# A Mamba and mixture-of-experts block: the experts' up product evicted by ScalarE and multiplied by GpSimd

## The reference, cut to what matters

```python
def reference(x, ...):            # x: (8, 1024, 256) float32
    # attention slot: a Mamba block on layernorm(x)
    xz = rms_norm(xn) @ in_proj_w; xb, z = split(xz)
    xc = silu(causal_conv4(xb) + conv_b)                     # 512 channels
    dt, B, C = split(xc @ x_proj_w); dt = softplus(dt @ dt_proj_w + dt_proj_b)
    h = exp(dt * A) * h + dt * B * xc                        # 16 states a channel, scanned over 1024 steps
    y = (sum_s(h * C) + xc * D) * silu(z)
    x = x + layernorm(y @ out_proj_w + residual)
    # FFN slot: 16 experts (256 -> 128 -> 256), 4 of 16 chosen by groups, weights sum to 1
    t = layernorm(x)
    g = einsum('th,eih->tei', t, gate_proj); u = einsum('th,eih->tei', t, up_proj)
    act = silu(g) * u
    y = einsum('teh,te->th', einsum('tei,ehi->teh', act, down_proj), combine)
    return x + layernorm(y)
```

## Time and profile before

| | us |
|---|---|
| median of 3 runs | 2711.35 |
| the profiled execution | 2710.63 |
| its span in the trace | 2708.8 |
| VectorE busy | 2437.7 |
| TensorE busy (matmul) | 2403.0 |
| ScalarE busy | 1632.9 |
| GpSimd busy | 1509.4 |

### The profile page before, as it was taken

How to read it: one execution, slowest core, us unless ns; L and a number is a source line. 1 busy time by engine, 2 the same in 40 slices (tenths; PEclk the granted TensorE clock), 3 DMA queues, 4 the chain that set the end, 5 groups by cost and what they waited for, 6 DMA issues and landing times.

```text
span 2708.8 us, 27117 instructions
## 1 busy us (share of the span) xinstructions
PE 2403.0 (89%) x8416; PEld 1179.6 (44%) x8416; DVE 2437.7 (90%) x3236; ACT 1632.9 (60%) x3312; POOL 1509.4 (56%) x546
## 2 busy tenths in 40 slices
PE   5556898999989899998989999898999989898988
PEld 2112354544535454443545445353544535443554
DVE  3999999999999999999999999999999999999642
ACT  5566566566766656666665666666566666644331
POOL 0555555556665555665555566555656655565521
PEclk9778999999999999999999999999999999999999
DMA  4342434435353353535344353533535343352321
GB/s 157 139 146 81 156 109 133 158 115 163 120 161 110 130 163 115 163 120 158 113 131 163 100 177 120 161 110 127 167 109 169 120 154 109 127 163 84 86 59 60
DMA packets 174923, 352.38 MB, mean 130 GB/s; under 512 B 16283, under 2 KB 81596, under 8 KB 166332
## 3 DMA queue, kind: packets, MB, share of 16 engines
q1 hardware_dynamic: 164700, 334.93, 37.1%
q0 software_dynamic: 10080, 15.73, 3.6%
HBM read 291.35 MB, written 51.38 MB: 127 GB/s over the span
## 4 chain that ended last, share of the span: by engine, by line
DVE 59%; issue 18%; ACT 14%; PE 8%; DMA 1%; POOL 0%; DVEq 0%; SPq 0%; ACTq 0%; POOLq 0%
DVE hs L1019 27%; DVE hs L1005 13%; DVE th L1129 5%; DVE th L1134 5%; PE Gp L479 2%; ACT DX L604 2%; PE Up L487 2%; PE MY L497 2%; DVE XC L972 2%; ACT dA L586 1%; ACT L586 1%; ACT XC L657 1%; ACT SZ L662 1%; ACT my L765 1%; ACT DX L727 1%
## 5 line engine op out<-in xcount | busy, mean ns | idle before, releaser
L897 POOL TENSOR_TENSOR hs<-hs,Cb 128x2048 f32<-128x2048 f32 x256 | 1170.9, 4574 | 165.9 <-DVE hs L1005 165.9
L586 ACT ACTIVATE dA<-dtr,A 128x512 f32<-128x512 f32 x1024 | 701.8, 690 | 830.7 <-DVE hs L1019 829.7
L877 POOL TENSOR_TENSOR th<-th,cmb 128x512 f32<-128x512 f32 x256 | 338.2, 1326 | 818.1 <-DVE hs L1005 712.6
L1019 DVE TENSOR_TENSOR_SCAN hs<-dA,carry,hs 128x512 f32<-128x512 f32 x512 | 628.2, 1264 | 19.9 <-ACT dA L586 19.6
L1019 DVE TENSOR_TENSOR_SCAN hs<-dA,hs 128x512 f32<-128x512 f32 x512 | 595.9, 1203 | 30.7 <-ACT dA L586 30.2
L479 PE MATMUL Gp<-x2T,Wgu 128*128 128x512 f32 x1024 | 528.1, 640 | 106.1 <-DVE th L1129 105.9
L1005 DVE TENSOR_TENSOR hs<-dxr,Bb 128x2048 f32<-128x2048 f32 x256 | 602.7, 2354 | 7.7 <-DMA dxr<-dx_d 7.5
L487 PE MATMUL Up<-x2T,Wgu 128*128 128x512 f32 x1024 | 492.6, 604 | 0.0
L497 PE MATMUL MY<-Wdn,th 128*128 128x256 f32 x2048 | 485.7, 381 | 0.8 <-POOL th L877 0.8
L497 PEld LDWEIGHTS MY<-Wdn,th 128*128 128x128 f32 x2048 | 383.3, 190 | 136.7 <-issue 91.9
L479 PEld LDWEIGHTS Gp<-x2T,Wgu 128*128 128x128 f32 x1024 | 180.8, 195 | 439.1 <-issue 246.3
(11 more groups left out here) (165 smaller groups left out, 1860.5 us busy)
## 6 DMA issues: line engine op xcount, KB each, us to landing
dtr<-dt_d SPq DMA_DIRECT2D x64, 1024.0 KB, 5.6
dxr<-dx_d SPq DMA_DIRECT2D x128, 512.0 KB, 7.3
cmb<-cm_d SPq DMA_DIRECT2D x256, 256.0 KB, 3.7
Wdn<-in_w_dn SPq DMA_DIRECT2D x256, 128.0 KB, 3.6
Bb<-bc_d SPq DMA_DIRECT2D x64, 256.0 KB, 3.1
Cb<-bc_d SPq DMA_DIRECT2D x64, 256.0 KB, 4.1
dt_d<-XB SPq DMA_DIRECT2D x15, 1024.0 KB, 4.3
dx_d<-DX SPq DMA_DIRECT2D x15, 1024.0 KB, 5.9
```

Of the source, the lines that this page charges most:

```text
L586: act.activation(dA[h % 2][:, :], dtr[:, M % 2, beta, :], ACT.Exp, scale=A[:, k:k + 1]).then_inc(s_dA, 1)
L877: pool.tensor_tensor(th[:, q % NTH, :], th[:, q % NTH, :], cmb[:, q % 2, :], ALU.mult).then_inc(m_a, 1)
L897: pool.tensor_tensor(hs[:, G % NH, :, :], hs[:, G % NH, :, :], Cb[:, s, :].unsqueeze(1).broadcast_to([P, NBETA, CH]), ALU.mult).then_inc(s ...
L1019: dve.tensor_tensor_scan(hv, dA[h % 2][:, :], hv, first, ALU.mult, ALU.add).then_inc(s_h, 1)
```

## The change

ScalarE now copies Up out of PSUM into a new SBUF tile Ub (`keep_up`, before `tanh`), and TensorE computes up before gate. `expert_up` leaves VectorE. `weigh` on GpSimd has two multiplies: Ub by the combine row, then th by Ub; it now handles the expert of group G-1, and where a group has two experts the second stands behind `read_out`. `load_cm` waits for the first of the two multiplies of the expert two before. To make room for Ub, several small tiles get smaller or are shared: `ln1` keeps four chunks, `z_s`, `z_w`, `z_nb` are those of the `p_` steps, `Ebias` is broadcast when read, and `to_y` is loaded into `hs`. The negative means of x are kept in `x_nm` and used again for the second norm, so `p_sums2` and its four row sums are gone. The z projections and their copies, `p_x2`, `e_norm` and `f_silu_z` move to other groups. The diff, cut to its core (the renamed arguments of `squares` and `shift` are left out):

```diff
-FILLS = ['b2', 'k2', 'r0', 'r1', 'b3', 'k3', 'z0', 'xp', 'x0', 'x1', 'rt', 'db', 'z1', 'ct', 'z2', 'z3', 'xT0', 'xT1', 'b0', 'b1']
+FILLS = ['b2', 'k2', 'r0', 'r1', 'b3', 'z0', 'k3', 'z1', 'xp', 'x0', 'x1', 'rt', 'z2', 'z3', 'db', 'ct', 'xT0', 'xT1', 'b0', 'b1']
...
-        ln1 = sb('ln1', [P, NC, 2, TB])
-        e_s = sb('e_s', [P, 3, TB])
+        ln1 = sb('ln1', [P, 4, 2, TB])
+        e_s = sb('e_s', [P, 2, TB])
+        x_nm = sb('x_nm', [P, 4, TB])
...
+        to_y = hs[:, NH - 1, 0, 0:P]
...
-        z_s = sb('z_s', [P, 3, TB])
-        z_w = sb('z_w', [P, 3, TB])
-        z_nb = sb('z_nb', [P, TB])
+        Ub = sb('Ub', [P, CH])
+        z_s, z_w, z_nb = (p_s, p_w, p_nb)
...
-                    sp.wait_ge(m_a, q - 1)
+                    sp.wait_ge(m_w, q - 1)
...
-            def gate(q):
+            def up(q):
                 c, e = divmod(q, NE)
                 if e == 0:
                     pe.wait_ge(p_act.sem, p_act.at(c, 'x2T1'))
+                if q >= 1:
+                    pe.wait_ge(m_us, q)
+                for k in range(KM):
+                    mm = pe.matmul(Up[:, :], Wgu[:, k, e, DE:2 * DE], x2T[:, c % 2, k, :], start=k == 0, stop=k == KM - 1)
+                mm.then_inc(m_u, 1)
+
+            def gate(q):
+                c, e = divmod(q, NE)
                 if q >= 1:
                     pe.wait_ge(m_v, q)
                 for k in range(KM):
                     mm = pe.matmul(Gp[:, :], Wgu[:, k, e, 0:DE], x2T[:, c % 2, k, :], start=k == 0, stop=k == KM - 1)
                 mm.then_inc(m_g, 1)
-
-            def up(q):
-                c, e = divmod(q, NE)
-                if q >= 1:
-                    pe.wait_ge(m_w, q)
-                for k in range(KM):
-                    mm = pe.matmul(Up[:, :], Wgu[:, k, e, DE:2 * DE], x2T[:, c % 2, k, :], start=k == 0, stop=k == KM - 1)
-                mm.then_inc(m_u, 1)
 
             def down(q):
...
+                    up(now[0])
                     gate(now[0])
-                    up(now[0])
-                if F and g in (0, 4, 6, 11):
-                    f_in(p, {0: 'b2', 4: 'b3', 6: 'z0', 11: 'z3'}[g])
+                if F and g in (0, 4, 6, 9):
+                    f_in(p, {0: 'b2', 4: 'b3', 6: 'z1', 9: 'z2'}[g])
                 if F and g in (1, 5):
...
-                if F and g == 9:
-                    f_dt(p)
...
-                if F and g in (9, 10):
-                    f_in(p, f'z{g - 8}')
+                if F and g == 4:
+                    f_in(p, 'z0')
+                if F and g == 9:
+                    f_in(p, 'z3')
+                    f_dt(p)
                 if in_e(p) and g == 13:
                     e_turn(p, 1)
                 if len(now) == 2:
+                    up(now[1])
                     gate(now[1])
...
+            def keep_up(q):
+                act.wait_ge(m_u, q + 1)
+                if q >= 1:
+                    act.wait_ge(m_a, q)
+                act.activation(Ub[:, :], Up[:, :], ACT.Copy).then_inc(m_us, 1)
...
-            def p_sums2(p):
+                means_squares(rn, p_s, p_s[:, 2, :], p_act, p - 1, 'rev1', dx_half).then_inc(p_act.sem, 1)
+
+            def p_squares2(p):
                 if p < NC:
                     act.wait_ge(x1_sum, 16 * p)
                 else:
                     act.wait_ge(x1_last, 1)
-                sums(x1[:, (p - 1) % 2, :, :], b_s, dx_half).then_inc(p_act.sem, 1)
-
-            def p_squares2(p):
-                squares(x1[:, (p - 1) % 2, :, :], b_s, p_act, p - 1, 'sum2', dx_half).then_inc(p_act.sem, 1)
+                act.wait_ge(e_dve.sem, e_dve.at(p - 1, 'w1'))
+                squares(x1[:, (p - 1) % 2, :, :], b_s, x_nm[:, (p - 1) % 4, :], dx_half).then_inc(p_act.sem, 1)
...
                 if len(experts_at(G - 1)) == 2:
+                    keep_up(experts_at(G - 1)[1])
                     tanh(experts_at(G - 1)[1])
...
-                if F and g in (10, 11):
-                    f_z(p, g - 9)
+                if F and g == 7:
+                    f_z(p, 1)
+                if R_ and g == 7:
+                    p_x2(p)
...
                 if experts_at(G):
+                    keep_up(experts_at(G)[0])
                     tanh(experts_at(G)[0])
...
-                    p_sums2(p)
                     p_squares2(p)
                 if R_ and g == 4:
                     p_ro(p)
-                if F and g in (6, 11):
-                    f_z(p, {6: 0, 11: 3}[g])
+                if F and g == 4:
+                    f_z(p, 0)
                 if F and g == 6:
                     f_silu(p)
-                if R_ and g == 6:
-                    p_x2(p)
                 if F and g == 7:
                     f_xd(p)
-                if in_e(p) and g == 7:
-                    e_norm(p + 2)
                 if R_ and g == 8:
                     p_x2T(p, 1)
+                if in_e(p) and g == 8:
+                    e_norm(p + 2)
                 if F and g == 9:
+                    f_z(p, 2)
+                    f_z(p, 3)
                     f_softplus(p)
                 if R_ and g == 10:
                     p_cmT(p)
@@ -861,7 +872,7 @@
                     z_my(p - 2)
                 if g == 12 and 0 <= p - 2 < NC:
                     z_norm(p - 2)
-                if F and g == 12:
+                if F and g == 10:
...
             def weigh(q):
+                pool.wait_ge(m_us, q + 1)
+                pool.wait_ge(ld_cm[q % 2], 16 * (q // 2 + 1))
+                pool.tensor_tensor(Ub[:, :], Ub[:, :], cmb[:, q % 2, :], ALU.mult).then_inc(m_w, 1)
                 pool.wait_ge(m_w, q + 1)
-                pool.wait_ge(ld_cm[q % 2], 16 * (q // 2 + 1))
-                pool.tensor_tensor(th[:, q % NTH, :], th[:, q % NTH, :], cmb[:, q % 2, :], ALU.mult).then_inc(m_a, 1)
+                pool.wait_ge(m_v, q + 1)
+                pool.tensor_tensor(th[:, q % NTH, :], th[:, q % NTH, :], Ub[:, :], ALU.mult).then_inc(m_a, 1)
...
-                for q in experts_at(G - 2):
-                    weigh(q)
+                done = experts_at(G - 1)
+                if done:
+                    weigh(done[0])
                 if 0 <= G - 1 < NGRP:
                     read_out(G - 1)
+                if len(done) == 2:
+                    weigh(done[1])
...
-            def expert_up(q):
-                dve.wait_ge(m_u, q + 1)
-                dve.wait_ge(m_v, q + 1)
-                dve.tensor_tensor(th[:, q % NTH, :], Up[:, :], th[:, q % NTH, :], ALU.mult).then_inc(m_w, 1)
...
                     expert_gate(done[0])
                 if S:
                     scan(G, 0)
-                if done:
-                    expert_up(done[0])
-                if S:
                     scan(G, 1)
                     scan(G, 2)
                 if len(done) == 2:
                     expert_gate(done[1])
                 if S:
                     scan(G, 3)
-                if len(done) == 2:
-                    expert_up(done[1])
```

More of the change, by code:

```diff
@@ L82, in at, with sandwich_kernel @@
         return c * self.per + (self.names if c else self.first).index(name) + 1
-def sandwich_kernel(nc, x, w_in, w_out, w_gu, w_dn, w_x, w_rt, cols, alog, ebias, consts, sel_dt, out):
+def sandwich_kernel(nc, x, w_in, w_out, w_gu, w_dn, w_x, w_rt, cols, alog, ebias, consts, sel_dt, w_y, out):
     with ExitStack() as ctx:
@@ L118, in sandwich_kernel @@
         Kdiag = sb('Kdiag', [P, len(PE_CONV) * TAPS, P])
-        Ebias = sb('Ebias', [P, TB * NE])
-        Cst = sb('Cst', [P, P + CB + NG * NG + TB * NE + P])
+        Ebias = sb('Ebias', [P, NE])
+        Cst = sb('Cst', [P, P + CB + NG * NG + TB * NE])
         SelDt = sb('SelDt', [2 * NS + 1, P])
@@ L203, in sandwich_kernel @@
         block = ctx.enter_context(nc.Block())
-        early = [(Cst, consts), (Cols, cols), (Win, w_in), (A, alog), (Wx, w_x), (SelDt, sel_dt)]
+        early = [(Cst, consts), (to_y, w_y), (Cols, cols), (Win, w_in), (A, alog), (Wx, w_x), (SelDt, sel_dt)]
         late = [(Wout, w_out), (Wrt, w_rt), (Ebias, ebias), (Wgu, w_gu)]
@@ L592, in tanh, with sums, squares, means_squares @@
                 act.activation(th[:, q % NTH, :], Gp[:, :], ACT.Tanh, scale=0.5).then_inc(m_th, 1)
-            def sums(x, s, to=None):
+            def keep_up(q):
[3 more added lines that the diff above has]
+                act.activation(Ub[:, :], Up[:, :], ACT.Copy).then_inc(m_us, 1)
+            def sums(x, s):
                 for b in range(TB):
-                    ins = act.activation(to[b] if to else x[:, b, :], x[:, b, :], ACT.Copy, accum_out=s[:, 0, b:b + 1])
+                    ins = act.activation(x[:, b, :], x[:, b, :], ACT.Copy, accum_out=s[:, 0, b:b + 1])
                 return ins
-            def squares(x, s, steps, c, n, waste):
+            def squares(x, s, nm, waste):
+                for b in range(TB):
+                    ins = act.activation(waste[b], x[:, b, :], ACT.Square, bias=nm[:, b:b + 1], accum_out=s[:, 1, b:b + 1])
+                return ins
```

(15 more changed lines are left out.)

31 lines of the change are left out of this document (14 added, 17 removed).

## The result

The changed kernel takes 3015.8 us (median of 4 runs, 3012.8 to 3017.5), against 2711.5 for the kernel before, timed beside it: a ratio of 1.112, interval 1.1104 to 1.1137. It is slower by 304 us, where 273 were forecast; the time lies 0.8 us above the forecast's own range (2955 to 3015) and inside the whole one (2945 to 3040). The profiled execution has a span of 3014.2 us (2708.8 before).

What follows compares the result with a forecast made beforehand. VectorE and GpSimd, taking turns on a shared port, bound the kernel. A chunk: 21.1 - 4.1 + 1.8 = +18.8; 14 chunks +263, two-expert groups +10: 2708.8 + 273 = 2982 span, 2984 us; range 2955 to 3015, whole 2945 to 3040.

Steps and rivals of the forecast that it cites:

- The turn-taking and its price: Quiet groups: VectorE's `inputs` finishes its work only after GpSimd's `read_out`; period 9.38 us, mean +1.32 a group, +21.1 a chunk.
- the signs: Trace after: `inputs` mean about 4 us, second multiply 1.3 to 1.4 behind, `inputs` 9.4 apart, chain over `read_out` and `inputs`.
- The rival without a lock: Quiet groups: no lock for these shapes, VectorE stays the bound, group 7.5 us, about 2575 us in all; 4%.
- The second eviction is free: ScalarE's added copy of Up, one a group: costs nothing; bounds -1 and +3 us a chunk.
- the rival in which ScalarE is late: Group 7: z copy and `p_x2` before decays and eviction make GpSimd start late, 3 us a chunk, 3026; 10%.
- Absorbed VectorE waits: VectorE's waits for ScalarE (3.6 us) and one `y_out` (0.5) now lie under GpSimd: -4.1 us a chunk.
- For fifteen experts that is free: SP may load it two groups ahead.: Combine rows of all but a chunk's first expert: needed one group earlier, at no cost.
- The first expert's rows: Group 11 of a chunk: GpSimd stands 1.8 us for the first expert's combine rows; bounds 0 and 5.3.
- the rival in which these rows cost 5 us a chunk: Weights come late, SP standing for `p_cmT`: 5 us a chunk instead of 1.8, +45, 3029; 8%.
- The ends: 26 groups without experts: 0; groups 251 to 255, two experts each: +10; tail after the last scan: 0, within 5.
- of no account: VectorE's small one-input operations: after a late GpSimd they start later and cost what they cost now.

Runs made afterwards that it cites:

- 64-column: Changed kernel with GpSimd's second multiply cut to 64 of 512 columns: 2861.5 us; with early combine rows from the chunk before, 2738.0 us.
- PSUM kernel: Changed kernel, `inputs` multiplying a PSUM constant instead of the B row, up computed into gate's bank: 2893.5 us; with early combine rows from the chunk before, 2744.1 us.
- new order: Kernel before with moved ScalarE and TensorE steps, smaller tables, no `p_sums2`; `expert_up` stays on VectorE, one GpSimd multiply: 2701.9 us (0.9965).
- The second multiply: Kernel before with its GpSimd expert multiply done twice, the second waiting for the first, nothing else changed: 2943.0 us (1.0856).
- old rows: Changed kernel with combine rows loaded one group earlier and taken from the chunk before, the first expert's too: 2948.3 us (1.0874).
- double eviction: Changed kernel with ScalarE evicting every up twice: 3044.4 us (1.1229); with early combine rows from the chunk before, 2952.8 us.

## Why the prediction was right, and where it was off

*The turn-taking and its price.* Right. Most of the signs came as promised: the second multiply 1.36 behind the first, `read_out` ending 7.2 after the last `inputs` (1504.68, with `inputs` ended at 1497.49, 0.08 ahead of 1497.57), 9.34 us a group for the 9.38 forecast, VectorE busier with less work. Two of the signs came out otherwise: the mean of `inputs` rose to 3.43 us and not to about 4, and the chain does not go over `read_out` (GpSimd has 3% of it, VectorE 67%), since an `inputs` that is held counts as busy and the chain runs through it. One reading of the rows was loose: the gate multiply of the earlier trace rows runs beside GpSimd's multiply; the operation with a PSUM input beside `read_out` there, besides the scans, is `expert_up`. The 64-column and the PSUM kernels show it from both sides: shorten GpSimd's instruction, and the group is shorter by as much; take the port away, and `inputs` is never held. The Trainium skill (SBUF — State Buffer, SBUF: two separate sides) has this as an exclusive lock on the ports that the two engines share, for a whole instruction; the trace agrees, with 4.34 us for an `inputs` of 2.28, ending 2.15 behind `read_out`.

*The rival without a lock* (2575) is out by those rows. *The second eviction is free:* nearly. A further one costs 4.5 us when rows are early, within the bounds of -14 to +42 that stood for the first; the rival in which ScalarE is late (3026) came near the measured time by its number, but not by its mechanism. All of GpSimd's 38.0 us of waits for the eviction lie behind the last scan, which starts at 2843.12; none is in group 7. The first of them:

```profile
2882.26 1.26 POOL L888 TENSOR_TENSOR Ub<-Ub,cmb 128x512 f32<-128x512 f32 x1 [18.11 <-ACT Ub L599]
```

*Absorbed VectorE waits.* 16 x 1.32 = 21.1 less 4.1 was to be +17.0 a chunk. Measured without the rows: 173.5 - 157.8 = 15.7, or 16.5 against the new order's own 157.0. Right to 1.3 us. Of this, 0.8 is the group itself, 16 times 9.33 for 9.38 (and for even chunks the prediction wrote 1.36 where 9.38 less 7.98 is 1.40).

*"For fifteen experts that is free: SP may load it two groups ahead."* This is the step that failed. The buffer is free two groups ahead, but SP's program has the load only one group ahead, behind a load of B that waits for `inputs` of the group before and behind 2 MB in the same queue. Issued at 1560.10, the rows were needed 8.7 later, and came after 10.6 (4.13 - 2.23 = 1.9 too late). Loading them a group earlier gave 39 us back. I had traced the queue for the first expert only, although the weighing was moved a group ahead for all sixteen.

*The first expert's rows.* 1.8 forecast, 1.46 read off the trace (5.86 - 4.40), and 29 us by the run that removes it, 1.9 a chunk with what else hung on it. Right, and so the rival in which these rows cost 5 us a chunk (3029) is out by its mechanism. Its amount, 45 us above the forecast, was nearly met all the same, since the rows of the other fifteen were late: the rows of all sixteen cost 4.2 a chunk.

*The ends.* The start costs 3.8 us, of which 2.7 are in the kernel with the new order alone; forecast 0. Behind group 245 it is 31.0 us for the 16.4 forecast, and 17.0 without late rows. There too the rows of the two-expert groups are what I had left out (waits of 2.6 to 2.9 us where two loads follow each other).

*Summed up.* The second multiply is worth 232 us by itself, the new order -10, late rows 67.5: 289.6 of the 304.3. A second eviction costs 4.5, so the first may be about as much of the remaining 15; no run isolates the other 10. About 7.5 of the 15 lie ahead of group 37: with old rows its x1 DMA comes at 400.3, where the second multiply (390.8) and the new order (2.0 later than before) would put it at 392.8. There the rows of the very first expert, which the kernels with old rows still await, hold GpSimd:

```profile
300.12 1.26 POOL L895 TENSOR_TENSOR Ub<-Ub,cmb 128x512 f32<-128x512 f32 x1 [8.38 <-DMA cmb<-cm_d]
```

In the kernel with the new order alone GpSimd idles 4.76 us before that group's `read_out`, so some 3.6 are the rows'. A candidate for what is left, not tried, is the single Ub, which ties the eviction to GpSimd's last multiply. The forecast of 2984 had 25 us for rows in it, so the missing 42 more than cover the 32 by which it was low; the other terms were too dear by some 10 together (224 groups at 9.38 for 9.33 are 11).

## What to carry to other kernels

Before work goes from VectorE to GpSimd, look whether the two already end together: where GpSimd's `read_out` ended at 1281.05 and VectorE's two-input multiply began at 1281.04, each microsecond added to GpSimd's group is a microsecond of the group, and what VectorE saves is worth nothing. When a consumer is moved ahead, follow each of its loads through the queue that issues it, for the common case and not for the special one alone: how early a buffer is free says nothing about when the load is issued, nor what it stands behind. And a change that fails can hold a part that pays: the new order alone is 9.6 us faster than before.

## What the runs showed that I had not expected

GpSimd holds back VectorE's small one-input operations too. In the PSUM kernel a multiply-add (TENSOR_SCALAR) of 4 columns took 2.12 us and ended at 1409.49, at the end of a `read_out` (1409.47). In the changed kernel the same operation has a mean of 1853 ns, and 192 in the kernel before, by its line in the groups:

```profile
L942 DVE TENSOR_SCALAR p_w<-b_s 128x4 f32<-128x4 f32 x16 | 3.1, 192 | 1.2 <-ACT DX L604 1.2
...
L959 DVE TENSOR_SCALAR p_w<-b_s 128x4 f32<-128x4 f32 x16 | 29.6, 1853 | 1.5 <-ACT DX L608 1.5
```

The prediction had called these operations of no account. The routing's TENSOR_SCALAR of 64 columns is held as well: 2064 ns in the mean, 223 before. For the sum the prediction holds: these are three operations a chunk, each held no longer than the next `inputs` would have been, and the chunk without late rows came out within 1.3 us of it. But they are no cheap filler beside a `read_out`. The Trainium skill (SBUF — State Buffer, Who interferes with whom) lists `tensor_scalar` among the operations that can enter a mode with both ports, and so be held; the trace agrees, with that 2.12.

The port can be lost in the other direction. Where VectorE was in first, `read_out` is the one that is long; the double eviction's GpSimd and VectorE:

```profile
1406.17 2.61 DVE L1024 TENSOR_TENSOR hs<-dxr,Bb 128x2048 f32<-128x2048 f32 x1
...
1406.60 6.55 POOL L913 TENSOR_TENSOR hs<-hs,Cb 128x2048 f32<-128x2048 f32 x1
```

`inputs` ends at 1408.78, `read_out` 4.37 behind it, as if it had started there. In the groups with two experts of the changed kernel a 512-column multiply that started at 2786.76 took 3.31 instead of 1.27, beside an `inputs` that ran from 2785.34 to 2788.94.

GpSimd's multiply costs 0.32, 0.73, 1.27 and 4.53 us for 64, 256, 512 and 2048 columns, and waiting for its own instruction before costs about 0.12: starts 1.36 apart with such a wait, 1.24 without one.
